# Accumulating transfers in place of GpSimd's subtractions, the fetch of the experts' rows and their additions

## The reference

```python
xn = layernorm(x)
# branch 1, a Mamba block: 4 heads, 256 inner channels, 16 states per channel
xin, z  = split(xn @ in_proj.T)
xc      = silu(conv4(xin));  dt, B, C = x_proj(xc) per head
delta   = softplus(dt_proj(dt) + bias);  A = -exp(A_log)
s_t     = s_{t-1} * exp(delta_t * A) + (delta_t * xc_t) * B_t
y_t     = sum over the states of s_t * C_t
out1    = ((y + xc * D) * silu(z)) @ out_proj.T
# branch 2, a mixture of 8 experts, top 1, at most 1024 tokens an expert
e, gate = argmax, max of softmax(xn @ Wg);  place = running count per expert
out2    = gate * (relu(xn @ W1[e] + b1[e]) @ W2[e] + b2[e])   # 0 for a token over the limit
return x + out1 + out2
```

## Time and profile before

| | us |
|---|---|
| median of three runs | 1085.64 |
| the profiled execution, its own time | 1085.05 |
| its span, first to last instruction | 1083.2 |
| busy DVE / PE / POOL / ACT | 1014.2 / 962.7 / 898.0 / 747.5 |

### The profile page before, as it was taken

How to read it: one execution, slowest core, us unless ns; L and a number is a source line. 1 busy time by engine, 2 the same in 40 slices (tenths; PEclk the granted TensorE clock), 3 DMA queues, 4 the chain that set the end, 5 groups by cost and what they waited for, 6 DMA issues and landing times.

```text
span 1083.2 us, 11968 instructions
## 1 busy us (share of the span) xinstructions
PE 962.7 (89%) x3521; PEld 440.5 (41%) x3521; DVE 1014.2 (94%) x1371; ACT 747.5 (69%) x1198; POOL 898.0 (83%) x783
## 2 busy tenths in 40 slices
PE   6978778799899999989999999999999999998785
PEld 3433223344444444434344444434444444443232
DVE  7789999999999999999999999999999999999995
ACT  5666465577887777786776877786787778786331
POOL 5458888997989898888888988888898888889874
PEclk8988998989999999999999999999999999999866
DMA  9584244344335342432533352243354233237821
GB/s 271 163 214 93 71 102 105 74 113 94 82 78 126 79 88 49 115 66 68 122 83 83 68 123 63 56 114 83 78 119 94 46 83 75 57 79 165 193 64 49
DMA packets 77452, 106.99 MB, mean 99 GB/s; under 512 B 8734, under 2 KB 46540, under 8 KB 77388
## 3 DMA queue, kind: packets, MB, share of 16 engines
q1 hardware_dynamic: 72944, 97.74, 40.5%
q0 software_dynamic: 4096, 8.46, 2.3%
q10 hardware_dynamic: 348, 0.03, 0.0%
HBM read 17.99 MB, written 21.10 MB: 36 GB/s over the span
## 4 chain that ended last, share of the span: by engine, by line
PE 35%; DVE 26%; issue 17%; ACT 15%; POOL 7%; DMA 0%; POOLq 0%; DVEq 0%; ACTq 0%
DVE u_sb L1020 11%; DVE s_sb L1075 8%; PE bank L1213 5%; PE bank L1250 4%; PE bank L1158 4%; PE bank L1265 4%; POOL s_sb L647 4%; PE bank L1243 4%; PE bank L1178 4%; ACT bank L863 3%; PE bank L1210 3%; PE bank L1169 2%; ACT L730 2%; ACT L726 2%; POOL moe L620 1%
## 5 line engine op out<-in xcount | busy, mean ns | idle before, releaser
L647 POOL TENSOR_TENSOR s_sb<-s_sb,c_of 128x512 f32<-128x512 f32 x488 | 625.0, 1290 | 122.2 <-DVE s_sb L1075 116.5
L1075 DVE TENSOR_TENSOR_SCAN s_sb<-bank,u_sb 128x512 f32<-128x512 f32 x512 | 620.9, 1213 | 14.2 <-ACT bank L863 14.0
L863 ACT ACTIVATE bank<-bank,a_neg 128x510 f32<-128x510 f32 x512 | 332.3, 663 | 213.4 <-PE bank L1250 211.7
L1020 DVE TENSOR_TENSOR u_sb<-bank,b_of 128x512 f32<-128x512 f32 x512 | 343.5, 671 | 24.9 <-PE bank L1243 23.8
L1243 PE MATMUL bank<-dsp,sel_d 128*128 128x512 f32 x512 | 326.3, 637 | 18.1 <-DVE u_sb L1020 16.7
L1250 PE MATMUL bank<-dsp,sel_d 128*128 128x512 f32 x512 | 228.2, 446 | 55.0 <-DVE s_sb L1075 51.9
L1243 PEld LDWEIGHTS bank<-dsp,sel_d 128*128 128x128 f32 x512 | 100.1, 195 | 194.3 <-DVE u_sb L1020 103.0
L1250 PEld LDWEIGHTS bank<-dsp,sel_d 128*128 128x128 f32 x512 | 100.2, 196 | 182.0 <-DVE s_sb L1075 136.6
L1265 PE MATMUL bank<-s_sb,con 128*32 128x512 f32 x1024 | 144.9, 639 | 17.4 <-POOL s_sb L647 13.4
L1158 PE MATMUL bank<-xnT,wx 128*128 128x512 f32 x256 | 133.8, 608 | 0.0
L653 POOL DMA_INDIRECT expert_in<-xn,put_at x64 | 70.1, 1096 | 11.6 <-issue 11.3
(11 more groups left out here) (143 smaller groups left out, 1014.2 us busy)
## 6 DMA issues: line engine op xcount, KB each, us to landing
b_of<-bc SPq DMA_DIRECT2D x64, 256.0 KB, 5.5
c_of<-bc SPq DMA_DIRECT2D x64, 256.0 KB, 5.9
dsp<-hi SPq DMA_DIRECT2D x64, 256.0 KB, 4.1
dsp<-dd SPq DMA_DIRECT2D x64, 256.0 KB, 4.7
expert_in<-fill SPq DMA_DIRECT2D x16, 260.0 KB, 5.4
xn<-expert_in SPq DMA_DIRECT2D x8, 520.0 KB, 5.3
moe<-fill SPq DMA_DIRECT2D x8, 512.0 KB, 6.8
xn<-L_ffn_W SPq DMA_DIRECT2D x16, 256.0 KB, 5.0
```

The lines of the kernel that those rows point to most:

```text
L647: pool.tensor_tensor(s_now, s_now, c_of[:, hf, hh, :], ALU.mult).then_inc(S["p_ready"], 1)
L863: act.activation(d, d, ACT.Exp, scale=a_neg[:, k:k + 1]).then_inc(S["decay_ready"], 1)
L1020: dve.tensor_tensor(u_sb[:, w % U_RING, :], du_ps[w % 2][:, :], b_of[:, hf, head_of(w), :], ALU.mult).then_inc(S["u_ready"], 1)
L1075: dve.tensor_tensor_scan(s_sb[:, w % S_RING, :], decay_of(w)[:, :], u_sb[:, w % U_RING, :], 0.0, ALU.mult, ALU.add).then_inc(S["scan_done" ...
```

## The change

The low part becomes `dd + (-hi)`: ACT writes the negative of the high part (`neg_hi`), POOL issues one transfer that adds `neg_hi` onto `dd` in SBUF, and the selector `K_I2` gets -1 for the rows of the high part. DVE's five low parts stay instructions of DVE. Their completions are counted apart (`low_made`). `back`, `load_back`, POOL's additions and the identity matmuls are gone: POOL issues 16 transfers that add rows of `moe` onto `acc` in SBUF, from slot 24 of chunk 14 every second slot to slot 22 of chunk 15, in the order of `MOE_ADD_ORDER`. For chunks 0 to 13 they come after `add_out`, for 14 and 15 before it, and there `add_out` waits for them. `moe` now has token 64*p + i for tile i and partition p, so that each partition reads 2 KB in one piece. In chunk 15 DVE makes the products of slots 28 to 31 and no others. SP issues all 16 stores after its loops.

```diff
-HELP = {0: 1, 1: 1, CHUNKS - 1: 1}
+HELP = {0: 1, 1: 1}
-MOE_ADD_FROM, MOE_ADD_STEP, MOE_ADDS = 15 * 32 + 1, 2, 14
+MOE_ADD_FROM, MOE_ADD_STEP = 14 * 32 + 24, 2
+MOE_ADD_ORDER = (0, 1, 2, 3, 4, 5, 14, 6, 7, 8, 9, 10, 11, 12, 13, 15)
...
+        def low_made(ch, hf):
+            halves = [(c, h) for c in range(ch + 1) for h in range(HALVES) if (c, h) <= (ch, hf)]
+            mine = parts_by_dve(ch, hf)
+            n = sum(parts_by_dve(*x) == mine for x in halves)
+            return (S["lo_by_dve"], n) if mine else (S["lo_by_dma"], 16 * n)
...
-            return w % QUADS < HELP.get(ch, 0)
+            return w % QUADS < HELP.get(ch, 0) or (ch == CHUNKS - 1 and w >= SLOTS - QUADS)
...
             def stack(ch, hf):
-                sp.wait_ge(S["lo_ready"], per_chunk(ch, 2, hf + 1))
+                sp.wait_ge(*low_made(ch, hf))
                 for hh in range(2):
-                    for n, part in enumerate((hi, lo)):
+                    for n, part in enumerate((neg_hi.bitcast(F32), dd)):
...
-            def load_back():
-                for n in range(4):
-                    sp.wait_ge(*half_put(EXP - 2 + n // 2, n % 2))
-                for g in range(TILES // GROUP):
-                    sp.dma_start(back[:, g * GROUP:(g + 1) * GROUP, :], ...
...
             def store_out(k):
-                if k < MOE_ADDS:
-                    sp.wait_ge(S["moe_added"], k + 1)
-                else:
-                    sp.wait_ge(*tile_read("outp", k, 0, 0))
+                sp.wait_ge(S[f"moe_added{k}"], 16)
+                sp.wait_ge(*tile_read("outp", k, 0, 0))
...
-            while stored[0] < CHUNKS:
-                store_out(stored[0])
-                stored[0] += 1
+            for k in range(CHUNKS):
+                store_out(k)
...
             def split_low(ch, hf):        # of POOL
                 pool.wait_ge(S["hi_ready"], per_chunk(ch, 2, hf + 1))
-                pool.tensor_tensor(lo, dd, hi.bitcast(F32), ALU.subtract).then_inc(S["lo_ready"], 1)
+                pool.dma_start(dd, neg_hi.bitcast(F32), accum_op=ALU.add).then_inc(S["lo_by_dma"], 16)
...
             def add_moe(k):
-                pool.wait_ge(*tile_read("outp", k, 0, 0))
-                pool.wait_ge(S[f"back_loaded{k * CT // GROUP}"], 16)
-                rows = acc[:, k * CT:(k + 1) * CT, :]
-                pool.tensor_tensor(rows, rows, back[:, k * CT:(k + 1) * CT, :], ALU.add).then_inc(S["moe_added"], 1)
+                if k == MOE_ADD_ORDER[0]:
+                    for n in range(4):
+                        pool.wait_ge(*half_put(EXP - 2 + n // 2, n % 2))
+                if k < CHUNKS - 2:
+                    pool.wait_ge(*tile_read("outp", k, 0, 0))
+                pool.dma_start(acc[:, k * CT:(k + 1) * CT, :],
+                               moe[0:TOK, :].rearrange("(p i) d -> p i d", p=P)[:, k * CT:(k + 1) * CT, :],
+                               accum_op=ALU.add).then_inc(S[f"moe_added{k}"], 16)
...
-                act.activation(hi, dd, ACT.Copy).then_inc(S["hi_ready"], 1)
+                act.activation(neg_hi, dd, ACT.Copy, scale=-1.0).then_inc(S["hi_ready"], 1)
...
                 dve.wait_ge(S["misc_pe"], tile_made("outp", ch, 0, 0))
+                if ch >= CHUNKS - 2:
+                    dve.wait_ge(S[f"moe_added{ch}"], 16)
...
-                    if more:
-                        mm = pe.matmul(t[:, i * P:(i + 1) * P], ident, back[:, ch * CT + i, :],
-                                       start=False, stop=True)
...
-    c[:, K_I2:K_I2 + 64] = (k[:, None] % 64) == np.arange(64)[None, :]
+    c[:, K_I2:K_I2 + 64] = np.where(k % 64 == np.arange(64)[:, None], np.where(k < 64, -1.0, 1.0), 0.0).T
-    c[:, K_TOK:K_TOK + TILES] = np.arange(TILES)[None, :] * P + k[:, None]
+    c[:, K_TOK:K_TOK + TILES] = np.arange(TILES)[None, :] + TILES * k[:, None]
```

More of the change, by code:

```diff
@@ L61 @@
 FIRST_DX = 12
-GROUP = 8
 EPS = 1e-5
@@ L348, in half_put @@
             return S[f"moe_put{n % 4}"], 16 * CT * (n // 4 + 1)
-        def moe_add_slot(k):
-            return MOE_ADD_FROM + MOE_ADD_STEP * k
         def wait(eng, name, value):
@@ L463, in stack @@
             def stack(ch, hf):
[L466 removed]
+                sp.wait_ge(*low_made(ch, hf))
                 for hh in range(2):
[L468 removed]
+                    for n, part in enumerate((neg_hi.bitcast(F32), dd)):
                         sp.dma_start(dsp[n * HD:(n + 1) * HD, hf, hh, :, :].bitcast(F32),
[L470 removed]
+                                     part[hh * HD:(hh + 1) * HD, :, :]).then_inc(S["stacked"], 16)
             def spread_bc(ch, hf):
@@ L664, in _ @@
                                 put_rows(x, q)
-                    if added < MOE_ADDS and t == moe_add_slot(added):
-                        add_moe(added)
-                        added += 1
+                    if t in moe_at:
+                        add_moe(moe_at[t])
         @block.scalar
@@ L1037, in split_low @@
                 dve.wait_ge(S["hi_ready"], per_chunk(ch, 2, hf + 1))
-                dve.tensor_tensor(lo, dd, hi.bitcast(F32), ALU.subtract).then_inc(S["lo_ready"], 1)
+                dve.tensor_tensor(dd, dd, neg_hi.bitcast(F32), ALU.add).then_inc(S["lo_by_dve"], 1)
             by_i = lambda a: a.rearrange("p (e i) -> p i e", e=EXP)
@@ L1062, in _, with product @@
             spread_u(0, 0)
+            def product(ch, w):
+                hf = w // UNITS
+                if not any(by_dve(ch, v) for v in range(hf * UNITS, w)):
+                    dve.wait_ge(*bc_loaded(ch, hf, "c"))
+                dve.wait_ge(S["scan_done"], per_chunk(ch, SLOTS, w + 1))
+                s_now = s_sb[:, w % S_RING, :]
+                dve.tensor_tensor(s_now, s_now, c_of[:, hf, head_of(w), :], ALU.mult).then_inc(S["p_dve"], 1)
             for ch in range(CHUNKS):
@@ L1077, in _ @@
                     if w > 0 and by_dve(ch, w - 1):
-                        if w - 1 in (0, UNITS):
-                            dve.wait_ge(*bc_loaded(ch, w // UNITS, "c"))
-                        dve.wait_ge(S["scan_done"], t)
-                        s_now = s_sb[:, (w - 1) % S_RING, :]
-                        dve.tensor_tensor(s_now, s_now, c_of[:, (w - 1) // UNITS, head_of(w - 1), :], ALU.mult
-                                          ).then_inc(S["p_dve"], 1)
+                        product(ch, w - 1)
                     for step in range(2):
@@ L1096, in _ @@
                             add_out(x.of)
+            product(CHUNKS - 1, SLOTS - 1)
             gate_half(CHUNKS - 1, 1, 0)
@@ L1186, in out_proj @@
                     pe.wait_ge(S["g_ready"], per_chunk(ch, 2, 2))
-                more = ch >= MOE_ADDS
-                if more and part == 0:
-                    pe.wait_ge(S[f"back_loaded{ch * CT // GROUP}"], 16)
                 for i in range(CT // 2 * part, CT // 2 * (part + 1)):
@@ L1192, in out_proj @@
                         mm = pe.matmul(t[:, i * P:(i + 1) * P], g_sb[:, hf, i * P:(i + 1) * P], wo[:, hf, :],
-                                       start=(hf == 0), stop=(hf == HALVES - 1 and not more))
-                    if more:
-                        mm = pe.matmul(t[:, i * P:(i + 1) * P], ident, back[:, ch * CT + i, :],
-                                       start=False, stop=True)
+                                       start=(hf == 0), stop=(hf == HALVES - 1))
                 if part == 1:
```

29 lines of the change are left out of this document (7 added, 22 removed).

## The result

The changed kernel takes 1073.81 us (median of four runs, 1072.36 to 1075.03) against 1085.64. The ratio is 0.9882, with a 95% interval of 0.9864 to 0.99: faster by 1.2%, where I had forecast 0.7%. Another five rounds of the same kernel (`after_again`) gave 1074.33 us, ratio 0.99 [0.9883, 0.9916]. The ratio times the median before is 1072.8 us, just under the low end of my range (1073). The profiled execution took 1074.44 us. Its span is 1072.6, so 10.6 us less than before. The medians differ by 11.8 us, since the profiled execution before was 0.6 us faster than its median and this one 0.6 slower; what follows accounts for the 10.6 of the spans.

A forecast was written before the change was run, and what follows sets the result against it. It took DVE (busy 94%, PE 89%) as the bound. Terms 3.8 - 1.5 + 4.2 + 0.8 - 0.5 + 1.7 + 0.9 - 2.0 gave 7.4 us of gain, so 1078.3 us, with an 8-in-10 range of 1073 to 1091.

The forecast's parts named there:

- four stalls behind POOL: Chunks 3, 6, 9, 12: PE's wait for POOL's product goes, 0.95 us each; gain 3.8 us, bounds 0 and 5.
- chunk 14, copy late for ACT: Low transfer of 4.6 us runs 1.5 us past its cover in chunk 14, stalling ACT; loss 1.5 us, bounds 0 and 4.
- seven products of DVE: Chunk 15: products at slots 0, 4, ..., 24 leave DVE, 0.60 us each; gain 4.2 us.
- the long product: Chunk 15: one DVE product took 1.471 us instead of 0.662 beside POOL's addition; that 0.8 us goes.
- last quad: Last four slots of chunk 15: DVE makes three products more; loss 0.5 us.
- identity matmuls at slot 19: Chunk 15: DVE's wait for spreading behind two projection tiles shortens without identity matmuls; gain 0.9 us.
- identity matmuls in the tail: Final four projection tiles run without identity matmuls, 0.43 us less each; gain 1.7 us.
- POOL's backlog in chunk 15: Sixteen issues of 1.17 us plus all products put POOL 4.0 us behind; loss 2.0 us.
- rival 1: Low transfer outlasts its cover; at 7 us twelve first halves and chunk 14 stall ACT; 1092 us, chance 0.17.
- rival 2: POOL's issue costs 1.7 us instead of 1.17, so POOL bounds the end; 1089 us, chance 0.13.
- rival 3: POOL's work only renamed, PE late anyway; only DVE's products and PE's matmuls count; 3.6 us, 1082, chance 0.2.
- rival 4: DVE in two-port mode keeps POOL from writing descriptors, stretching issues of 1.01 by 0.66 us; 1089 us, chance 0.02.

The follow-up runs named there:

- experiment 4: Kernel before without the identity matmuls of chunks 14 and 15, the experts' rows left out of the output; 1083.77 us, ratio 0.9973.
- experiment 1: Kernel before with only the low part's subtraction on POOL made an accumulating transfer; 1078.82 us, ratio 0.993.
- experiment 5: Kernel before with POOL's low-part subtraction over half the columns and no accumulating transfer; 1080.15 us, ratio 0.9939.
- experiment 6: Changed kernel with a plain 256 KB transfer issued by POOL ahead of each low transfer from chunk 3 on; 1083.33 us, ratio 0.9975.
- experiment 7: Changed kernel with the last low part (chunk 15, second half) made by an instruction of POOL; 1075.08 us, ratio 0.9898.
- experiment 8: Changed kernel with no addition issued between slot 30 of chunk 14 and slot 8 of chunk 15; 1074.97 us, ratio 0.989.
- experiment 9: Changed kernel with the edits of experiment 7 and experiment 8 together; 1073.38 us, ratio 0.989.
- experiment 11: Changed kernel with each of the sixteen additions split into two transfers of half the size; 1082.85 us, ratio 0.9966.
- f3_both: The kernel of experiment 9: changed kernel, last low part by POOL and additions kept apart from it; 1073.38 us, ratio 0.989.
- experiment 2: Changed kernel with the low parts put back as subtractions of POOL and DVE; 1078.85 us, ratio 0.9929.
- experiment 12: Changed kernel with POOL's 27 low transfers as plain copies instead of additions; one execution, 1076.37 us.
- experiment 3: Changed kernel with DVE making eight products in chunk 15 as before; 1076.76 us, ratio 0.9915.
- experiment 10: Changed kernel measured once more, no edit; 1074.33 us, ratio 0.99.

## Why the prediction was right or wrong

By the terms of the sum, in us of gain:

| term | forecast | measured |
|---|---|---|
| four stalls behind POOL | 3.8 | 5.25 |
| chunk 14, copy late for ACT | -1.5 | -0.27, and not by ACT |
| seven products of DVE | 4.2 | 4.2 |
| the long product | 0.8 | 0.81 |
| last quad (-0.58 at slot 30, 0.33 ahead of PE's last sum) | -0.5 | -0.25 |
| identity matmuls at slot 19 | 0.9 | 0.78, the clock with them |
| identity matmuls in the tail | 1.7 | 1.40 (experiment 4: 1.46) |
| POOL's backlog in chunk 15 | -2.0 | 0 |
| copy late for PE, slot 15 | none | -1.24 |
| small losses in chunk 15 (slots 0, 11, 27) | none | -0.63 |
| start and the rest | none | 0.6 |
| sum | 7.4 | 10.6 |

The direction and all mechanisms but one were right; that one is the copy that PE waits for. Five terms, taken from single rows of before, hit within 0.3 us, one of them by luck (slot 19). Three steps failed, all in the size of a term.

*"I count 4 x 0.95."* I priced the stall by the two scans right behind it. PE, late by 1.24 us, also gave its next spreadings late, and DVE lost another 0.36 us over slots 14 and 15. Experiments 1 and 5 show 1.31 and 1.07 us for a relief of 1.41 (2.37 less 0.96) and 1.10: POOL's relief comes back one to one until the wait is used up. My upper bound of 5, "if PE keeps the whole 1.24 us", was the case, and the measured 5.25 is a little above even that.

*"A stall of ACT reaches DVE less its lead, an estimate of 0.6 us."* The transfer was sized rightly (4.62 against 4.6). The lead was not: 2.13 us of idle time don't reach DVE in chunk 14, and of 3.81 in experiment 6 1.65 do (at slot 28), which leaves a lead of 2.1 to 2.2 us. But that is chunk 14's. In chunk 11 the lead was 0.15 us and in chunk 6 nothing (experiments 6 to 9 and 11), so one number for all chunks was wrong both ways. The 0.27 us that are lost are 0.70 at slot 30 less 0.42 at slot 31, and experiment 5, where nothing lands late, shows the same pair. There PE's softplus sums stand ahead of the spreading, and they run at half the clock: the window rows have a granted clock of 0.66 for 994 to 997 us, so much of it at 1.2 GHz, and 1.00 at the same slots before, where the like stretch (994.1 to 997.5 us) came two to three slots earlier. The lines (timeline after) are

```profile
993.71 1.91 PE L1169 MATMUL bank<-sp_e,con 128*128 128x512 f32 x2
995.41 1.33 PE L1169 MATMUL bank<-sp_r,con 128*128 128x512 f32 x2
996.18 0.79 PE L1228 MATMUL bank<-dsp,sel_d 128*128 128x512 f32 x1
```

and a pair of the same kind takes 1.02 us at 999.30, with the clock at 1.00.

*"Fourteen of 1.270 us become sixteen issues of 1.17 ... a loss of 2.0 us. It is steep."* The steepness was right, the size wrong. In `f3_both` two products and an issue repeat every 3.42 us:

```profile
1021.39 0.87 POOL L618 DMA_DIRECT2D acc<-moe  x1
1021.99 2.88 POOL L638 TENSOR_TENSOR s_sb<-s_sb,c_of 128x512 f32<-128x512 f32 x2
1024.81 0.87 POOL L618 DMA_DIRECT2D acc<-moe  x1
```

The product starts 0.60 us after the issue and is some 0.3 longer, so an issue costs at most 0.86 us (3.42 less 2 x 1.28) and not 1.17. At most, since 3.42 is also DVE's 2 x 1.71; by the ends of experiment 11 it is 0.89, so 0.82 to 0.89. My own text said that at 1.0 us the loss is nothing. I had taken the indirect write's price for it (1.16 or 1.17: its 9.2 us of idle time fall on 60 writes and not on 56), and the lower bound of 0.7 was nearer. I also looked for the damage at the wrong receiver: not at POOL's products, but at the copy. *"Second halves have over twice the first halves' cover"* holds where the transfer takes 5.7 to 7.8 us, as in the other second halves. In chunk 15 it stands in POOL's queue among additions that land after a median of 6.1 us, and takes 9.1. Experiments 2, 7 and 9, without that low transfer, and 8, with no additions around it, have no wait for the copy.

Slot 19 is right in the first trace by luck of the clock. Over the traces it gains 0.1 (experiments 8 and 12), 0.66 to 0.92 (the change and experiments 1, 4, 5, 6) and 1.97 us (experiments 2, 3, 7, 9, 10); in experiment 11 it loses 1.40, behind POOL. Experiments 1 and 5 still have the identity matmuls and gain 0.66 and 0.92, so the 0.78 can't be put down to them. The rows of windows (start to end, length, busy us with counts of PE, PEld, DVE, ACT, POOL, granted clock, DMA share, GB/s) show the sum and projection tiles before the spreading of slot 20: before, after, and in experiment 2.

```profile
1040.00:1043.00 3.00, 3.00 (x12) 0.90 (x13) 3.00 (x5) 0.66 (x1) 3.00 (x3) 0.50 0.26 79
```

```profile
1033.00:1036.00 3.00, 3.00 (x15) 1.41 (x15) 3.00 (x4) 0.66 (x1) 3.00 (x4) 0.60 1.12 298
```

```profile
1037.00:1040.00 3.00, 2.37 (x16) 1.12 (x16) 3.00 (x5) 0.94 (x2) 3.00 (x5) 1.00 0.90 180
```

At 1.2 GHz (0.50) PE takes 1.93 us for a sum and at 2.4 GHz (1.00) 1.06, and whether such a stretch lies on that knot or beside it differs from trace to trace. These up to 1.9 us belong in a range. The start-up varies too: chunks 0 to 2 end between 266.3 and 268.8 us in the seven traces whose program up to there is the changed kernel's.

*The rivals.* 1: refuted for this kernel (transfer 4.6 in most first halves, 5.43 at most, decisive above 5.1 to 6.3), shown as a mechanism by experiments 6 and 8. 2: refuted (0.96 us for the low transfer), its mechanism shown by experiment 11. 3: refuted by experiment 5. 4: its price, 1.67 us an issue, is refuted, since an issue costs 0.82 to 0.89 us beside a DVE that is 94% busy; whether DVE is ever in the mode that the rule speaks of no run shows.

What stays open: why slots 0, 11 and 27 of chunk 15 lose 0.31, 0.16 and 0.16 us (slot 0 does so in experiment 5 too, by 0.27), whether `f3_both` is faster than the change by the clock, and a run that forces the late transfers.

## What to carry to other kernels

Price a stall by all slots until the landmarks of both sides run even again, not by the first gap: an engine that is late stays late for its next deliveries. Moving work from an engine to its DMA queue is cheap as long as the queue is empty; ask for each queued transfer what stands in front of it, and keep the one that somebody waits for apart from the bulk. And measure the slack behind a new transfer by the wait's end at the engine that sets the pace, since ACT's idle time of 2.1 us cost nothing in one chunk, and 0.9 us cost 2.7 in another, two thirds of it at PE, which had sat idle behind ACT and then ran at half its clock. That happened in both traces where ACT idled 0.9 us or more in chunk 6, and was not forced by a run of its own.
